# The transposed inverse of a delta-rule chunk: built by a second set of small matmuls instead of by a transpose on VectorE

## The reference: what is computed

```
def step(S, inp):
    q_t, k_t, v_t, g_t, b_t = inp
    Sk = einsum('bhkv,bhk->bhv', S, k_t)
    delta = einsum('bhv,bhk->bhkv', v_t, k_t) - einsum('bhv,bhk->bhkv', Sk, k_t)
    S = exp(g_t)[..., None, None] * S + b_t[..., None, None] * delta
    o_t = einsum('bhkv,bhk->bhv', S, q_t)
    return (S, o_t)
```

## Time and profile before

| | us |
|---|---|
| median of three runs | 4481.34 |
| the profiled execution, its own time | 4485.19 |
| its span | 4483.4 |
| TensorE busy in the span | 4193.2 (94%) |
| VectorE busy | 3277.2 (73%) |
| ScalarE busy | 1912.7 (43%) |
| GpSimd busy | 1037.1 (23%) |

### The profile page before, as it was taken

How to read it: one execution, slowest core, us unless ns; L and a number is a source line. 1 busy time by engine, 2 the same in 40 slices (tenths; PEclk the granted TensorE clock), 3 DMA queues, 4 the chain that set the end, 5 groups by cost and what they waited for, 6 DMA issues and landing times. The chain is left out here.

```text
span 4483.4 us, 135200 instructions
## 1 busy us (share of the span) xinstructions
PE 4193.2 (94%) x56335; PEld 2629.6 (59%) x56335; DVE 3277.2 (73%) x5448; ACT 1912.7 (43%) x2685; POOL 1037.1 (23%) x1042
## 2 busy tenths in 40 slices
PE   5999699999999999999788799999999999999998
PEld 4444389888989888877566344444444444444443
DVE  4899766666666666644499688787878787878886
ACT  2888511111111111113344266565656565656654
POOL 1000135444444444420277500000000000000000
PEclk9999899999999999999898699999999999999999
DMA  3534511211111111122444400000000000000000
GB/s 127 178 116 131 162 52 59 65 57 62 61 58 61 58 61 58 61 69 88 137 109 111 96 9 9 12 5 19 5 19 5 19 5 11 12 9 14 10 14 9
DMA packets 261588, 249.08 MB, mean 56 GB/s; under 512 B 51712, under 2 KB 230016, under 8 KB 260256
## 3 DMA queue, kind: packets, MB, share of 16 engines
q1 hardware_dynamic: 240528, 209.39, 15.6%
q0 software_dynamic: 6144, 16.79, 1.2%
q10 hardware_dynamic: 14352, 14.55, 1.0%
HBM read 135.27 MB, written 105.38 MB: 54 GB/s over the span
## 5 line engine op out<-in xcount | busy, mean ns | idle before, releaser
L2211 DVE TENSOR_REDUCE part_max<-p_m 128x1 f32<-128x512 f32 x2118 | 1363.2, 685 | 379.4 <-PE p_m L2053 371.9
L2193 ACT ACTIVATE prob<-p_s 128x1024 f32<-128x1024 f32 x1024 | 1047.6, 1023 | 749.6 <-PE p_s L2117 747.5
L2072 PE MATMUL p_o<-prob,v_one 128*64 128x512 f32 x4096 | 1055.0, 593 | 3.9 <-ACT prob L2193 0.5
L2053 PE MATMUL p_m<-keys,queries 96*64 96x512 f16 x4236 | 661.2, 387 | 28.0 <-DMA keys<-parts_d 20.4
L2117 PE MATMUL p_s<-queries,keys 97*64 97x512 f16 x4096 | 619.1, 380 | 0.0
L2117 PEld LDWEIGHTS p_s<-queries,keys 97*64 97x64 f16 x4096 | 228.0, 109 | 599.3 <-issue 593.9
L2053 PEld LDWEIGHTS p_m<-keys,queries 96*64 96x64 f16 x4236 | 238.6, 108 | 311.5 <-DVE part_max L2211 56.4
L2021 POOL TENSOR_TENSOR attn<-o_num,o_inv 32x512 f32<-32x512 f32 x64 | 80.9, 1265 | 1458.7 <-DVE o_inv L2230 1452.3
L2072 PEld LDWEIGHTS p_o<-prob,v_one 128*64 128x64 f32 x4096 | 287.5, 136 | 162.7 <-issue 15.8
L848 PE MATMUL pd_pre<-inv,step 64*64 64x64 f32 x10240 | 347.7, 220 | 7.0 <-POOL inv L1151 2.8
L590 PE MATMUL p_proj<-xn_t_all,proj_w_sb 128*128 128x512 f32 x768 | 337.8, 596 | 7.7 <-PEq L2356 7.7
(11 more groups left out here) (243 smaller groups left out, 6445.1 us busy)
## 6 DMA issues: line engine op xcount, KB each, us to landing
q_d<-conv_q SPq DMA_DIRECT2D x16, 1024.0 KB, 5.0
v_d<-conv_v SPq DMA_DIRECT2D x16, 1024.0 KB, 5.0
k_d<-conv_k SPq DMA_DIRECT2D x16, 1024.0 KB, 6.5
sums<-sums_d SPq DMA_DIRECT2D x128, 128.0 KB, 3.0
k_t<-k_d SPq DMA_DIRECT2D x32, 512.0 KB, 4.5
q_t<-q_d SPq DMA_DIRECT2D x32, 512.0 KB, 3.5
v_t<-v_d SPq DMA_DIRECT2D x32, 512.0 KB, 3.4
slots_d<-zero ACTq DMA_DIRECT2D x1, 10112.0 KB, 32.5
```

The lines of the kernel that those rows point to most:

```text
L2053: last = te.matmul(p_m[k % 2][x * HALF:(x + 1) * HALF, :], queries[0:ROW, p, hh, at:at + HALF], keys[0:ROW, 2 * p + hh, kb * BLK:(kb + 1) ...
L2072: product = te.matmul(p_o[64 * hh:64 * hh + VW, :], g.v_one[:, j, p, hh:hh + 2, :].rearrange("p a d -> p (a d)"), prob[:, j % 2, hh, :], s ...
L2193: a.activation(prob[:, j % 2], p_s[j % 2][:], ACT.Exp, scale=SCORE_SCALE).then_inc(exp_d, 1)
L2211: v.tensor_reduce(part_max[:, hh * SUB + sub, kb:kb + 1], p_m[k % 2][:], AX.X, ALU.max).then_inc(red_d, 1)
```

## The change

The stream transpose is gone. In its place TensorE forms the transposed increment of the inverse with a further batch, `low`, whose operands are those of `up` with their places changed, and adds it up over levels 1 to 4 in the PSUM tile `pd_low`. VectorE's `add_low` then adds `low_1` to that tile and writes `inv_low`. The order on TensorE changes too: per level it was up 0, up 1, the step of `post`, half 0, half 1; it is now low 0, up 0, low 1, up 1, half 0, the step of `post`, half 1.

```diff
--- before.py
+++ after.py
@@ -745,7 +745,7 @@
     proj_d, tok_d = sem("proj"), sem("tok")
     diff_d, min_d, grow_d, rel_d, relb_d, qg_d, kg_d = (sem2(s) for s in ("diff", "min", "grow", "rel", "relb", "qg", "kg"))
     kk_d, qk_d, upper_d, att_d, off_d, inv1_d, row_d, rows_d = (sem2(s) for s in ("kk", "qk", "upper", "att", "off", "inv1", "row", "rows"))
-    half_d, step_d, lowc_d, upmm_d, up_d = (sem2(s) for s in ("half", "step", "lowc", "upmm", "up"))
+    half_d, step_d, lowmm_d, lowc_d, upmm_d, up_d = (sem2(s) for s in ("half", "step", "lowmm", "lowc", "upmm", "up"))
     g.used_sems = sems
 
     def heads():
@@ -878,10 +878,19 @@
             wait_each(pe, freed, (lowc_d[x], n.level[k]))
             each(p_pre[x], of(upper[x]), of(low_1[x] if k == 1 else inv_low[x])).then_inc(half_d[x], 1)
 
+        def low(n, x, k):
+            if k == 1:
+                wait_each(pe, (inv1_d[x], n.now), (step_d[x], n.level[k]))
+            else:
+                wait_each(pe, (step_d[x], n.level[k]))
+            for p, hs in heads():
+                last = te.matmul(p_low[x][hs, p, :], inv[x][hs, p, :], step[x][hs, p, :], start=k == 1 and p == 0, stop=k == NL - 1,
+                                 skip_group_check=True)
+            last.then_inc(lowmm_d[x], 2 if k == 1 else 1)
+
         def up(n, x, k):
-            if k == 1:
-                wait_each(pe, (inv1_d[x], n.now))
-            wait_each(pe, (step_d[x], n.level[k]))
+            if k == NL:
+                wait_each(pe, (step_d[x], n.level[k]))
             each(p_pre[x], of(step[x]), of(inv[x])).then_inc(upmm_d[x], 1)
 
         def residual(n, x):
@@ -944,12 +953,13 @@
                 residual(post, 1)
             for k in range(1, NL):
                 if pre is not None:
-                    up(pre, 0, k)
-                    up(pre, 1, k)
+                    for x in range(2):
+                        low(pre, x, k)
+                        up(pre, x, k)
+                    half(pre, 0, k + 1)
                 if post is not None and k <= 3:
                     (updates, outputs, new_state)[k - 1](post, 1)
                 if pre is not None:
-                    half(pre, 0, k + 1)
                     half(pre, 1, k + 1)
             if post is not None:
                 project(post, range(0, NPAIR // 2))
@@ -1076,9 +1086,9 @@
             dve.wait_ge(half_d[x], n.level[k])
             v.tensor_tensor(step[x][:], p_pre[x][:], over_pairs(masks[:, k - 1, :]), ALU.mult).then_inc(step_d[x], 1)
 
-        def turn_low(n, x, k):
-            dve.wait_ge(up_d[x], n.level[k])
-            v.transpose(inv_low[x][:].rearrange("p n t -> p (n t)"), inv[x][:].rearrange("p n t -> p (n t)")).then_inc(lowc_d[x], 1)
+        def add_low(n, x, k):
+            dve.wait_ge(lowmm_d[x], n.level[k + 1])
+            v.tensor_tensor(inv_low[x][:], low_1[x][:], p_low[x][:], ALU.add).then_inc(lowc_d[x], 1)
 
         def add_up(n, x, k):
             if k == 1:
@@ -1107,8 +1117,8 @@
             for k in range(1, NL):
                 if pre is not None:
                     for x in range(2):
+                        add_low(pre, x, k)
                         add_up(pre, x, k)
-                        turn_low(pre, x, k)
                     if k == NL - 1 and ahead is not None:
                         decays(ahead, 0)
                     mask_step(pre, 0, k + 1)
```

## The result

The changed kernel takes 4650.51 us (median of four, 4649.33 to 4652.89), the kernel before on the same chip 4483.26. That is 167 us slower. The ratio over all fifteen fast runs of the changed kernel on record is 1.0378, interval 1.0365 to 1.0390, which would be 169 us. Forecast were 4658 and +177. The profiled execution of the changed kernel has a span of 4658.0, at the long end: the spans of those fifteen runs lie between 4643.0 and 4660.0.

What follows compares the result with a forecast made beforehand. TensorE, busy 1337 of the delta rule's 1415 us, was taken as the bound. 5.5 us per couple over 31 iterations (169), 3 for the first and 5 for fetching gave +177, 4658 us; range 4640 to 4680, for 8 in 10 4625 to 4705.

Steps and rivals of the forecast that it cites:

- the batch price: Each of 256 `low` batches on TensorE costs 0.935 us, 7.48 us per couple, before old waits are filled.
- The rival with `low` beside `up`: `low` runs on idle array parts, VectorE sets the pace: not slower, 4475 to 4485 us; chance 0.03.
- The give-back: The new batches partly fill TensorE's old waits for VectorE in the levels, 2.0 us a couple.
- Level 3: Level with the `new_state` step of `post`: from 5.11 to 6.55 us, +1.44.
- level 4: Level with nothing between the halves: from 5.22 to 5.97 us, +0.75, with 0.21 of wait.
- the way back to TensorE: From the end of VectorE's operation to the TensorE batch that waits for it: 0.15 us.
- Level 1: Level with the `updates` step of `post`, laid out like level 3: about 5.2 us before, +1.4.
- Level 2: Level with two batches of `post` and no wait to give back: 7.18 us before, +1.87 if the pause stays.
- The rival in which the waits stay: Old waits stay and the whole batch price is paid: 239 us, 4720, with fetching 4742; chance 0.08.
- the pause in `outputs`: TensorE pause in level 2, beside GpSimd's indirect DMAs: 7.18 us for six batches of 5.61; expected to stay.
- Instruction fetch: Some 55 more instruction packets for TensorE, taken as 5 us; as a binding rival 4675 to 4695, chance 0.09.
- the first iteration: The iteration without `post`: levels go from 5.09 to 5.83 us, four times 0.74, 3 us.

Runs made afterwards that it cites:

- a kernel with next to nothing left to fill: The changed kernel with one extra batch of 16 matmuls per level, behind `up` 1, whose result nobody reads; 4758.4 us, ratio 1.0619.
- the new order alone: The kernel before, with transposes and without `low`, but with the step of `post` between the two halves; 4508.4 us, ratio 1.0063.
- the scatter in level 4: The kernel before, but GpSimd's scatter waits until the mask of level 4 is made; 4511.4 us, ratio 1.0073.
- the projection: The kernel before with the first piece of the output projection put in level 4 between `up` 1 and `half` 0; 4454.0 us, ratio 0.9945.
- the last kernel: The kernel before with that projection piece in level 4, `half` 0 ahead of `outputs` in level 2, and `residual` ahead of `keys_keys`; 4440.9 us, ratio 0.9917.

## Why the prediction was right

**The step that carries it, the batch price, held.** I took 0.935 us and full price on TensorE's path; the batches of `low` come 0.933 apart, and in a kernel with next to nothing left to fill, four extra ones a couple cost 110 us of 120. The rival with `low` beside `up` needed under 0.25 and is out.

**The give-back held in kind and in size.** All of the waits for `inv_low` that the profile names went (36.2 us to none). Level 3 was forecast at 6.55 and took 6.53, level 4 at 5.97 and took 5.88, with 0.13 of wait for `half` 1 instead of 0.21. The difference is not in the reading: the last addition began at 4.06, where I had 4.05. It is the way back to TensorE, which I had at 0.15 from rows behind a transpose and which is 0.05 behind an addition. Level 1 was laid out like level 3 and takes 6.53 without a scattered pause. Level 2 was laid out at 7.18 + 1.87 = 9.05 and took 8.89. The rival in which the waits stay is out.

**The pause stayed, as said, in another place.** I called it the pause in `outputs` and let it stay because the scatter still follows the same level's update. The reason held, but not the place. In the changed kernel the scatter meets TensorE before `outputs`, in `up` 1 of level 2. GpSimd's second indirect DMA starts at 1458.11, and TensorE shows

```profile
1458.88 0.39 PE L848 MATMUL pd_pre<-inv,step 64*64 64x64 f32 x6 [0.37 <-issue]
1459.63 0.93 PE L848 MATMUL pd_pre<-inv,step 64*64 64x64 f32 x24 [0.37 <-issue]
```

It goes with the scatter, not with the batch. It cost about the same: level 2 has 1.43 more than its eight batches, before 1.56 more than its six. So the sum hardly noticed; that the new place would be no dearer I had not shown.

**Instruction fetch was a guess of the right order.** The packets were 64, not 55: 1.05 MB for 16384 instructions is 64 bytes each, where the mean of the whole program is 55. TensorE's idle time named "issue", in the stage, was 37.4 us before and 47.1 after in the profiled executions, 10 more, and that of the changed kernel's second profile was 38.6. So it grew by 1 or by 10 us, by execution, and what of it is fetching no run here shows. I had 5.

**The sum.** Forecast +177, measured +167. Of the 10 us, level 4 gives 31 x 0.07 = 2 (it grew by 0.68, not 0.75), level 2 31 x 0.14 = 4 (1.73, not 1.87), the first iteration 2 (40.44 to 41.79 us, 1.3 and not 3), and the fetch term up to 5. The scattered pauses change by as much from run to run: the mean steady couple took 49.97 us in one profile of the changed kernel and 49.48 in the other, 14 us over 30 couples, against 44.25 before. A couple was forecast to grow by 5.5 and grew by 5.7 and 5.2. So how near the total came is in part chance; that it came within some 15 us is not. One slip in the range: by the prediction's own terms its lower end of 4640 is 4.9 us a couple, not 5.0.

**Where I was wrong** is in the layouts of the experiments, the larger misses all at the same spot. Level 2 was treated as a sum of its batches and a fixed pause. The pause can be shared with a wait (the new order alone, +29 instead of +60), or it can lengthen one (the scatter in level 4, +32 instead of -30), and with the wait it can bring the clock down, a cost that I had not laid out at all.

## What to carry to other kernels

Before work is moved from one engine to another, ask which of the two ends the stage. Here a transpose of 0.7 us on an engine with spare time became a batch of 0.93 us on the one that was busy 94% of the stage, and only what TensorE had waited came back. Lay the stage out level by level with measured distances between batches; a wait can be filled once, and it is cheaper to fill it with work that has to be done anyway (the projection, -25 us) than to do away with it by new work (+167 us). Before a stall is moved into a wait, look at what the wait is for: if the work or the signal that ends it falls in the stall, the two add. Read a delay between engines behind the same kind of instruction as the one that will stand there.

## What was not expected of the hardware

GpSimd's scatter, a copy and two indirect DMAs per couple, stops TensorE's stream for about 1.4 us (level 2 of 7.16 against 5.77), and the start of a VectorE instruction that waits for TensorE came 1.4 us late beside it; by leaving it out the kernel gained 41.7 us. What it shares with TensorE, no run here shows.

TensorE's next batch starts 0.15 us after the end of a VectorE transpose that it waited for, and 0.05 us after that of an addition.

A pause with a wait right behind it brought TensorE to its lower clock for about 3 us in 15 of 30 couples, and cost some 19 us, in a kernel whose granted clock was otherwise 1.00 there. It did so in the last kernel once.
